# Regrouping loads, transposes and norms at five places of a fused two-layer kernel

## Chip, cores and metric
The kernel runs on one NeuronCore of one Trainium2 chip. The metric is the device time of one execution in microseconds. TensorE is PE in the profile, VectorE is DVE, ScalarE is ACT, GpSimd is POOL and the DMA-issuing SyncE is SP.

## What is computed
Four blocks in a row, each with a residual connection, all in float32, on 2 sequences of 512 tokens of width 256:

```python
x = hidden_states                       # (2, 512, 256)
x = x + delta_rule_attention(layernorm(x))      # 16 heads of 16; q, k, v = silu(conv4(x @ W)); scan over time
x = x + moe0(layernorm(x))              # 8 experts of 176, top 2, plus a shared part of 704
x = x + attention1(layernorm(x))        # 16 query heads, 2 key heads of 128, rotary, tanh soft cap, causal
x = x + moe1(layernorm(x))              # 16 experts of 176, top 6
```

`layernorm` is `(x - mean) / sqrt(var + 1e-5)` over the 256 columns. An expert is `silu(x @ gate) * (x @ up) @ down`.

## The kernel before, in words
All engines run programs written out by hand, with semaphores between them; no planner orders anything, so the order within each engine's function is the order of execution. The 1024 tokens are 8 tiles of 128 rows (`NT`), a half is 4 tiles.

**Start.** `Norm` normalises the tokens. `Norm.dve` does the statistics, the reciprocal and the scaling tile by tile, and each scaled tile counts up `ln_xn`. `Norm.pe_turn` transposes a half on TensorE: for each of the two column blocks (`KD`) four transposes into one bank, all behind one wait for the four tiles. `Norm.act_turn` copies the two banks to `xnT`. Then `attn0.pe` runs the projections (`proj`, L2115): `proj(0)`, `proj(1)`, the second half's `pe_turn`, the betas (L2122), `proj(2)` and on. `Attn0.act` (`pads`) and `Attn0.dve` (`taps`) do the convolution on the projections.

**First mixture.** The shared part and the routed part are separate. The shared part has 17 iterations M (`gate_up` L1281/L1297, `silu` L1552/L1554, `mul` L1674/L1677, `down` L1320). M = 0 to 7 come before the routed blocks, M = `F0B` = 8 to 16 (`F0END` = 17) behind them. Their weights are tiles L of `w_gu` (256 KB) and `w_dn` (128 KB) in a ring of `NW` = 5; SP loads them with `load_gu` (L1063, or two halves at L1061 for the last tile) and `load_dn` (L1070). L = 8 to 11 (`F0B` to `NL0` - 1) are those that M = 8 and later need. The routed part has `NB` = 23 blocks j of 128 token rows. SP reads a row number from `tab` (L1144) and fetches the block's rows from DRAM into `xg`, a ring of three (L1145); block j is fetched once block j - 3 is transposed. TensorE per block: `block_turn` (L953), `block_gate_up` (L967), `block_hidden` (L978), `block_down` (L989); in its loop step j it turns block j + 2, does gate and up of j + 1, hidden of j and down of j - 1. In SP's loop all four weight tiles, nine DMAs, are issued behind block j = 2 and ahead of block 3.

**The norm behind the first mixture.** Norm pieces e = 4 and 5 (`ln_stats`, `ln_std`, `ln_norm`, `ln_turn`, `ln_evac`) are placed among M = 12 to 16. ScalarE's square root (`ln_std`, L490) and its silu use different function tables; `ready` (L1559) runs a one-element activation ahead of time so that the table load comes there.

**Second attention.** 32 heads n (`NH`). TensorE per head: scores (L1461), `turn` of the head before (L1369), `queries` of the next (L1345), `project` of the head before (L1359), probabilities times values (L1502). `owners(J)` reads two offsets for pair J of the second mixture into PE's registers (L778).

**Second mixture.** `NP1` = 32 pairs J of half blocks: `pair_turn` (L728), `pair_hidden` (L756), `pair_gate_up` (L744), `pair_down` (L770) on TensorE, `pair_copy_gu`, `pair_x`, `pair_silu`, `pair_y` on ScalarE. Norm pieces 10 and 11 (for the second half of the tokens) are placed among the pairs; then 25 dense iterations from M = `F1` = 17 follow.

Of the kernel before, what the change touches and what calls it, by code (L numbers as in the profile page):

```python
# [7 lines left out]
P = 128  # L8
# [3 lines left out]
KD = DIM // P  # L12
# [34 lines left out]
ARENA = 39300  # L47
# [21 lines left out]
def build(nc, io):  # L69
    ctx = ExitStack()  # L70
    with ctx:
# [6 lines left out]
        bank = [ctx.enter_context(nc.psum_tensor(f"bank{i}", [P, 512], F32)) for i in range(8)]  # L78
# [20 lines left out]
        arena = sb("arena", [P, ARENA])  # L99
# [7 lines left out]
        s_eps = sem("s_eps")  # L107
# [7 lines left out]
        ln_std, ln_xn, ln_tp, ln_xT = (sem(f"ln_{n}") for n in ("std", "xn", "tp", "xT"))  # L115

        class Norm:
# [29 lines left out]
                    nc.scalar.copy(xnT[:, k, half * HALF:(half + 1) * HALF], bank[q][:]).then_inc(ln_xT, 1)  # L147

            def pe_turn(self, pe, half):
                pe.wait_ge(ln_xn, 4 * (half + 1))  # L150
                for k in range(KD):
                    q = half * KD + k
                    for j in range(4):
                        mm = nc.tensor.transpose(bank[q][:, j * P:(j + 1) * P],
                                                 xn[:, half * 4 + j, k * P:(k + 1) * P], ident[:])
                    mm.then_inc(ln_tp, 1)

        norm = Norm()
        rest = make_rest(nc, io, sem, sb, arena, bank, dict(
            x_sb=x_sb, xn=xn, xnT=xnT, ident=ident, causal_t=causal_t, stats=stats, mv=mv, std=std, rstd=rstd,  # L160
# [26 lines left out]
        @block.gpsimd  # L187
        def _(pool):
            pool.memset(eps_ln[:], EPS).then_inc(s_eps, 1)
            pool.memset(warm[:, 0:2], 0.0).then_inc(s_eps, 1)  # L190
            attn0.pool(pool)
            rest.pool(pool)

# [9 lines left out]

        @block.tensor
        def _(pe):
            pe.wait_ge(s_id.sem, 16)
            norm.pe_turn(pe, 0)
            attn0.pe(pe)
            rest.pe(pe, attn0)
# [8 lines left out]
def make_rest(nc, io, sem, sb, arena, bank, g):  # L218
# [27 lines left out]
    NGRP, NH = BATCH * HKV, BATCH * HQ  # L246
# [229 lines left out]
    class Rest:  # L476
# [632 lines left out]
        def sp(self, sp, attn0):  # L1109
# [31 lines left out]
            for j in range(NB):  # L1141
                if j >= 3:
                    sp.wait_ge(s_bx, j - 2)
                row = sp.value_load(tab[0:1, 0, j:j + 1], min_val=0, max_val=MOE[0][0] * CAP)  # L1144
                sp.dma_start(xg[:, j % 3, :], rows_in[bass.ds(row, P), :]).then_inc(s_cb[j % 3], 16)  # L1145
                if j == 2:
                    for L in range(F0B, F0B + NW - 1):
                        self.load_gu(sp, L)
                        self.load_dn(sp, L)
                if j == 5:  # L1150
                    for L in range(F0B + NW - 1, NL0):
                        self.load_gu(sp, L)
                        self.load_dn(sp, L)
            for n in range(NH):
                if n < NH - 2:
                    sp.wait_ge(s_q, n + 1)
# [215 lines left out]
        def pe(self, pe, attn0):  # L1372
# [66 lines left out]
            for n in range(NH):  # L1439
                grp = n // REP  # L1440
                pe.wait_ge(s_rot, rots(f"q{n}"))
                if n in (4, 5):
                    self.ln_turn(pe, 2 + n)
                if n in K_AT:
                    self.keys(pe, K_AT[n], b_q)
                if n in V_AT:
                    self.values(pe, V_AT[n], b_q)
                if n == 19:
                    self.ln_turn(pe, 9)
                if n == 20:  # L1450
                    self.logits(pe, 2)
                pe.wait_ge(s_qr, rot[f"q{n}"] + 1)
                if n == 0:
                    pe.wait_ge(s_ve, 1)
                for sbank, kts in enumerate([[0], [1, 3], [2]]):
                    if n:
                        pe.wait_ge(s_th, n * 3 - 2 + sbank)
                    for kt in kts:
                        w = SEQ - kt * P
                        o = P_OFF[kt] - 512 * sbank  # L1460
                        mm = nc.tensor.matmul(b_s[sbank][:, o:o + w], kT[:, grp, kt * P:(kt + 1) * P],  # L1461
                                              qr[:, kt * P:SEQ], start=True, stop=True, skip_group_check=True)
                    mm.then_inc(s_sc, 1)
                if n == 18:
                    self.ln_turn(pe, 8)
                if n == 23:
                    self.places1(pe, 0)
                if n:
                    self.turn(pe, n - 1)
                if n in (4, 5):  # L1470
                    pe.wait_ge(ln_xT, 4 + n + 3)
                if n in K_AT:
                    pe.wait_ge(s_rot, rots(f"k{K_AT[n]}"))
                if n in V_AT:
                    pe.wait_ge(s_ve, V_AT[n] + 1)
                if n == 18:
                    pe.wait_ge(ln_xT, 4 + 9)
                if n == 19:
                    pe.wait_ge(ln_xT, 4 + 10)
                if n == 20:  # L1480
                    pe.wait_ge(s_sub, 3)
                if n == 23:
                    pe.wait_ge(s_pl, RD1[0])
                if n < NH - 1:
                    self.queries(pe, n + 1)
                else:
                    self.pair_turn(pe, 0)
                if n == NH - 2:
                    offs = [owners(J) for J in range(3)]
                if n:  # L1490
                    self.project(pe, n - 1)
                else:
                    self.values(pe, 1, b_y[1])
                if n == NH - 1:
                    self.pair_turn(pe, 1)
                pe.wait_ge(s_p, n * 2 + 2)
                for pair in range(2):
                    for t in range(2):
                        qb = pair * 2 + t
                        for kt in range(qb + 1):  # L1500
                            o = P_OFF[kt] + (qb - kt) * P
                            mm = nc.tensor.matmul(b_o[pair][:, t * (DH + 1):(t + 1) * (DH + 1)],  # L1502
                                                  pr[:, o:o + P], v[:, grp, kt, :],
                                                  start=(kt == 0), stop=(kt == qb))
                    mm.then_inc(s_pv, 1)
# [59 lines left out]
        def act(self, act, attn0):  # L1565
# [29 lines left out]
            for M in range(F0B + 1, F0END):  # L1595
                self.silu(act, M)
                if M == F0END - 4:
                    self.ready(ACT.Sqrt)
                    self.ln_std(act, 4)
                if M == F0END - 3:  # L1600
                    self.ready(ACT.Sqrt)
                    self.ln_std(act, 5)
                if M == F0END - 2:
                    self.ln_evac(act, 4)
            self.ln_evac(act, 5)
            self.ready(ACT.Tanh)
            self.v_evac(act, 0, b_s[0])
# [31 lines left out]
            for J in range(NP1):  # L1639
# [4 lines left out]
                    self.pair_silu(act, J + 1)  # L1644
                if J:
                    self.pair_y(act, J - 1)
                if J == 5:
                    self.ln_std(act, 10)
                if J == 6:
                    self.ln_std(act, 11)  # L1650
                if J == 9:
                    self.ln_evac(act, 10)
# [53 lines left out]
        def dve(self, dve, attn0):  # L1706
# [38 lines left out]
            for M in range(F0B, F0END):  # L1745
# [8 lines left out]
                if M == F0END - 3:  # L1754
                    self.add_rows(dve, 1)
                    self.ln_stats(dve, 5)
                if M == F0END - 2:
                    self.ln_norm(dve, 5)
            dve.wait_ge(s_cs, 48)
            dve.wait_ge(s_k, 1)  # L1760
# [1230 lines left out]
```

## Time and profile before

| | |
|---|---|
| median of 3 runs | 836.53 us (835.92 to 839.29) |
| the profiled execution | 836.49 us |
| its span, first to last instruction | 834.7 us |
| mean granted TensorE clock | 0.991 |
| PE busy | 787.2 us (94%) |
| DVE busy | 482.1 us (58%) |
| ACT busy | 360.4 us (43%) |
| POOL busy | 218.4 us (26%) |

The span is the time inside the core; the rest of the execution's time, 1.8 us, lies around it. Busy time of PE counts matmul records; one float32 matmul is two records here, a transpose is one. "Idle before <- X" in a row is idle time of that engine just ahead of the instruction and what ended it.

### The profile page before, as it was taken

What the parts mean: (1) busy time and instruction counts of PE and PEld (TensorE: products, weight loads), DVE (VectorE), ACT (ScalarE), POOL (GpSimd) and SP (SyncE); (2) the same over time, 40 slices, a digit from 0 to 9 for tenths busy, and PEclk for the clock granted to TensorE, in tenths of its full rate; (3) what the DMA queues carried; (4) which work ended last, traced back from release to release, by engine and by line L of the source; (5) the groups of instructions that cost most, each with busy time, mean ns of one, the idle gap of its engine ahead of it and who ended that gap; (6) DMA issues with size and microseconds to landing.
All of it is one profiled execution on the core that took longest, in us unless ns stands there. A gap on an engine that the chain in (4) does not pass through costs nothing.

```text
span 834.7 us, 14393 instructions
## 1 busy us (share of the span) xinstructions
PE 787.2 (94%) x4825; PEld 545.6 (65%) x4825; DVE 482.1 (58%) x1167; ACT 360.4 (43%) x755; POOL 218.4 (26%) x318
## 2 busy tenths in 40 slices
PE   5988799879989998899999999999999999999998
PEld 3576566665657776577777777777764545455557
DVE  5999866766622225865564575967645463324443
ACT  3988777646213324343323343232347666211111
POOL 3644654111610015111211211217712333200000
PEclk9998999999999999999999999999999999999999
DMA  4001790083343312034443232223333433284431
GB/s 145 2 1 29 220 309 1 3 209 101 102 139 103 106 60 82 13 103 135 122 131 93 69 102 69 61 54 99 119 71 114 141 96 110 88 278 126 127 126 50
DMA packets 95807, 85.72 MB, mean 103 GB/s; under 512 B 34792, under 2 KB 84456, under 8 KB 95736
## 3 DMA queue, kind: packets, MB, share of 16 engines
q1 hardware_dynamic: 88200, 70.05, 28.9%
q0 software_dynamic: 4224, 11.74, 4.0%
q10 hardware_dynamic: 3312, 3.02, 1.1%
q8 instruction: 41, 0.67, 0.3%
q14 instruction: 30, 0.25, 0.1%
HBM read 57.02 MB, written 26.71 MB: 100 GB/s over the span
## 4 chain that ended last, share of the span: by engine, by line
PE 79%; DVE 10%; ACT 6%; issue 3%; DMA 1%; SPq 1%; POOL 0%; ACTq 0%; DVEq 0%; POOLq 0%
PE bank L1502 9%; PE bank L1461 8%; PE bank L1320 7%; PE bank L1359 7%; PE bank L1345 6%; PE bank L1281 6%; PE bank L1297 6%; PE bank L744 4%; PE bank L770 3%; PE bank L967 3%; PE bank L2330 3%; PE bank L989 2%; ACT arena L2387 2%; PE bank L2287 2%; PE bank L2314 2%
## 5 line engine op out<-in xcount | busy, mean ns | idle before, releaser
L1619 ACT ACTIVATE arena<-bank 128x512 f32<-128x512 f32 (+1 forms) x96 | 46.8, 525 | 142.7 <-PE bank L1461 142.7
L1243 POOL TENSOR_TENSOR arena<-arena,causal_t 128x256 f32<-128x256 f32 x64 | 45.3, 729 | 208.5 <-ACT arena L1624 207.5
L1502 PEld LDWEIGHTS bank<-arena 128*128 128x128 f32 x640 | 76.2, 191 | 3.9 <-POOL arena L1243 2.3
L1502 PE MATMUL bank<-arena 128*128 128x129 f32 x640 | 77.0, 275 | 1.5 <-POOL arena L1243 1.5
L1461 PE MATMUL bank<-arena 128*128 128x512 f32 (+3 forms) x256 | 74.5, 434 | 1.4 <-DVE arena L1697 1.4
L1554 ACT ACTIVATE arena<-bank 128x512 f32<-128x512 f32 (+1 forms) x39 | 20.2, 520 | 120.7 <-PE bank L1281 111.9
L1320 PE MATMUL bank<-arena 128*128 128x256 f32 (+1 forms) x272 | 66.2, 382 | 3.5 <-DVE arena L1677 3.4
L1281 PE MATMUL bank<-xnT,arena 128*128 128x512 f32 (+1 forms) x168 | 65.9, 514 | 0.0
L1320 PEld LDWEIGHTS bank<-arena 128*128 128x128 f32 (+1 forms) x272 | 50.9, 190 | 21.8 <-issue 10.8
L1359 PEld LDWEIGHTS bank<-arena 128*128 128x128 f32 x256 | 48.3, 190 | 21.6 <-issue 13.6
L1359 PE MATMUL bank<-arena 128*128 128x256 f32 x256 | 60.8, 380 | 1.4 <-issue 0.9
L1345 PE MATMUL bank<-arena 128*128 128x512 f32 x128 | 60.5, 595 | 1.2 <-DVE arena L1695 0.8
L1297 PE MATMUL bank<-xnT,arena 128*128 128x512 f32 (+1 forms) x156 | 61.5, 516 | 0.0
L1461 PEld LDWEIGHTS bank<-arena 128*128 128x128 f32 x256 | 41.3, 191 | 27.0 <-issue 18.5
L1679 DVE TENSOR_TENSOR arena<-arena,bank 128x512 f32<-128x512 f32 (+1 forms) x25 | 15.6, 623 | 68.0 <-PE bank L1297 68.0
L851 POOL DMA_INDIRECT ret<-arena,ridx x32 | 30.7, 960 | 77.0 <-ACT arena L818 60.3
L1693 DVE TENSOR_TENSOR arena<-bank,arena 64x512 f32<-64x512 f32 x36 | 25.0, 693 | 36.7 <-PE bank L1345 26.2
L1297 PEld LDWEIGHTS bank<-xnT,arena 128*128 128x128 f32 x156 | 29.6, 190 | 25.3 <-issue 23.8
L744 PE MATMUL bank<-arena 128*64 (+1 forms) x256 | 44.9, 472 | 0.0
L1704 DVE COPY arena<-bank 128x256 f32<-128x256 f32 x64 | 24.1, 418 | 34.5 <-PE bank L1369 30.8
L2330 PE MATMUL bank<-w,arena 128*128 128x128 f32 x248 | 35.5, 286 | 7.2 <-DVE w L2863 3.3
L1281 PEld LDWEIGHTS bank<-xnT,arena 128*128 128x128 f32 x168 | 31.2, 190 | 16.5 <-issue 14.0
(297 smaller groups left out, 1489.6 us busy)
## 6 DMA issues: line engine op xcount, KB each, us to landing
arena<-in_w_gu SPq DMA_DIRECT2D x44, 256.0 KB, 3.3
rows_in<-place SPq DMA_DIRECT2D x5, 1664.0 KB, 14.6
arena<-in_w_dn SPq DMA_DIRECT2D x34, 128.0 KB, 3.5
rows<-arena SPq DMA_DIRECT2D x8, 544.0 KB, 4.4
arena<-in_w_dn SPq DMA_DIRECT2D x24, 176.0 KB
arena<-in_wq SPq DMA_DIRECT2D x32, 128.0 KB
arena<-in_wo SPq DMA_DIRECT2D x32, 128.0 KB
arena<-rows SPq DMA_DIRECT2D x32, 128.0 KB, 2.0
```

Of the source, the lines that this page charges most:

```text
L744: mm = nc.tensor.matmul(p_gu[J % 2][u * HR:(u + 1) * HR, 0:2 * FE].rearrange("p (y n) -> p y n", y=2), pxT[:, J % 2, k, u * HR:(u + 1) * H ...
L851: nc.gpsimd.indirect_dma_start(ret[h], bass.IndirectOffsetOnAxis(ap=ridx[:, h, j:j + 1], axis=0), py[J % NY], None).then_inc(s_ret, 16)
L1243: nc.gpsimd.tensor_tensor(blocks, blocks, causal_t[:].unsqueeze(1).to_broadcast([P, 2, P]), ALU.mult).then_inc(s_p, 1)
L1281: mm = nc.tensor.matmul(ring(M)[0][:, 0:n], (w_gu, w_gu1)[s][:, slot_of(M), k * P:(k + 1) * P], xnT[:, k, cols], start=(k == 0), stop=(k = ...
L1297: mm = nc.tensor.matmul(ring(M)[1][:, 0:n], (w_gu, w_gu1)[s][:, slot_of(M), (KD + k) * P:(KD + k + 1) * P], xnT[:, k, cols], start=(k == 0 ...
L1320: mm = nc.tensor.matmul(Y[s][half][l // 2][:, (l % 2) * DIM:(l % 2 + 1) * DIM], (hh, hh1)[s][rows, M % 3, j * P:(j + 1) * P], (w_dn, w_dn1 ...
L1345: mm = nc.tensor.matmul(b_q[:], wq[:, n % 2, k, :], xnT2[:, k, b * SEQ:(b + 1) * SEQ], start=(k == 0), stop=(k == KD - 1))
L1359: mm = nc.tensor.matmul(b_y[t // 2][:, (t % 2) * DIM:(t % 2 + 1) * DIM], oT[:, t * P:(t + 1) * P], wo[:, n % 2, :], start=first and t % 2 ...
L1461: mm = nc.tensor.matmul(b_s[sbank][:, o:o + w], kT[:, grp, kt * P:(kt + 1) * P], qr[:, kt * P:SEQ], start=True, stop=True, skip_group_chec ...
L1502: mm = nc.tensor.matmul(b_o[pair][:, t * (DH + 1):(t + 1) * (DH + 1)], pr[:, o:o + P], v[:, grp, kt, :], start=(kt == 0), stop=(kt == qb))
L1619: nc.scalar.activation(th[:, sbank * 512:sbank * 512 + w], b_s[sbank][:, 0:w], ACT.Tanh, scale=SCALE / SOFTCAP).then_inc(s_th, 1)
L2330: mm = nc.tensor.matmul(sacc[h][:, j * P:(j + 1) * P], kq[:, u, hq * P:(hq + 1) * P], ub[s][:, hq, :], start=False, stop=True, skip_group_ ...
```

## The change
It has five parts. (1) At the start GpSimd also zeroes 384 columns of the arena (`still`), and TensorE runs nine 128x256 matmuls on them into bank 7, which nobody reads, ahead of everything else. (2) `Norm.pe_turn` waits for each tile singly and transposes both its column blocks, in place of waiting for four. (3) SP issues the four weight tiles for M = 8 and later one behind each of the blocks j = 6, 7, 8 and 9, in place of all behind block 2. (4) On TensorE the offsets of the pairs 0, 1 and 2 are read in heads 28, 29 and 30, one pair each, in place of all in head 30. (5) The square roots are moved: that of piece 5 from M = 14 to behind M = 16's silu, and `ln_norm(5)` to behind mul(16); those of pieces 10 and 11 both stand in J = 6, in place of J = 5 and 6.

```diff
             def pe_turn(self, pe, half):
-                pe.wait_ge(ln_xn, 4 * (half + 1))
-                for k in range(KD):
-                    q = half * KD + k
-                    for j in range(4):
-                        mm = nc.tensor.transpose(bank[q][:, j * P:(j + 1) * P],
+                for j in range(4):
+                    pe.wait_ge(ln_xn, 4 * half + j + 1)
+                    for k in range(KD):
+                        mm = nc.tensor.transpose(bank[half * KD + k][:, j * P:(j + 1) * P],
                                                  xn[:, half * 4 + j, k * P:(k + 1) * P], ident[:])
-                    mm.then_inc(ln_tp, 1)
-
+                        if j == 3:
+                            mm.then_inc(ln_tp, 1)
+
+        still = arena[:, ARENA - 3 * P:]
...
             pool.memset(warm[:, 0:2], 0.0).then_inc(s_eps, 1)
+            pool.memset(still, 0.0).then_inc(s_eps, 1)
...
         def _(pe):
+            pe.wait_ge(s_eps, 3)
+            for _ in range(9):
+                nc.tensor.matmul(bank[7][:, 0:256], still[:, 0:P], still[:, P:3 * P], start=True, stop=True)
             pe.wait_ge(s_id.sem, 16)
...
                 sp.dma_start(xg[:, j % 3, :], rows_in[bass.ds(row, P), :]).then_inc(s_cb[j % 3], 16)
-                if j == 2:
-                    for L in range(F0B, F0B + NW - 1):
-                        self.load_gu(sp, L)
-                        self.load_dn(sp, L)
-                if j == 5:
-                    for L in range(F0B + NW - 1, NL0):
-                        self.load_gu(sp, L)
-                        self.load_dn(sp, L)
+                if F0B <= F0B + j - 6 < NL0:
+                    self.load_gu(sp, F0B + j - 6)
+                    self.load_dn(sp, F0B + j - 6)
...
-                if n == NH - 2:
-                    offs = [owners(J) for J in range(3)]
+                if n == NH - 4:
+                    offs = []
+                if n >= NH - 4 and len(offs) < 3:
+                    offs.append(owners(len(offs)))
...
                 if M == F0END - 4:
                     self.ready(ACT.Sqrt)
                     self.ln_std(act, 4)
-                if M == F0END - 3:
+                if M == F0END - 2:
+                    self.ln_evac(act, 4)
+                if M == F0END - 1:
                     self.ready(ACT.Sqrt)
                     self.ln_std(act, 5)
-                if M == F0END - 2:
-                    self.ln_evac(act, 4)
             self.ln_evac(act, 5)
...
-                if J == 5:
+                if J == 6:
                     self.ln_std(act, 10)
-                if J == 6:
                     self.ln_std(act, 11)
...
                     self.ln_stats(dve, 5)
-                if M == F0END - 2:
+                if M == F0END - 1:
                     self.ln_norm(dve, 5)
```

## Rows read from the trace of the kernel before

**Rows 1.** The page's chain of work that ended last, by engine.
```profile
PE 79%; DVE 10%; ACT 6%; issue 3%; DMA 1%; SPq 1%; POOL 0%; ACTq 0%; DVEq 0%; POOLq 0%
```
**Rows 2.** Timeline, TensorE alone, 7 to 26 us: start, us.
```profile
7.83 1.94 PE L154 MATMUL bank<-ident,xn 128*128 128x128 f32 x8 [7.83 <-DVE xn L135]
10.44 5.56 PE L2115 MATMUL bank<-xnT,w 128*128 128x512 f32 x8 [0.68 <-ACT xnT L147]
15.84 1.04 PE L154 MATMUL bank<-ident,xn 128*128 128x128 f32 x8
...
18.42 7.97 PE L2115 MATMUL bank<-xnT,w 128*128 128x512 f32 x18
```
**Rows 3.** Timeline, all engines, 0 to 22 us.
```profile
0.81 0.32 POOL L2576 MEMSET place<- 128x256 f32 x1
...
3.09 0.43 SPq L177 DMA_DIRECT2D w<-in_w  x1
...
6.30 1.38 DVE L135 TENSOR_SCALAR xn<-x_sb,mv,rstd 128x256 f32<-128x256 f32 x4
...
8.95 0.58 ACT L147 COPY xnT<-bank 128x512 f32<-128x512 f32 x1 [2.90 <-PE bank L154]
```
**Rows 4.** DMA issues, 0 to 30 us: KB, median us to landing.
```profile
w<-in_w SPq DMA_DIRECT2D x1, 512.0 KB, 6.3
```
**Rows 5.** Timeline, all engines, 226 to 262 us.
```profile
241.61 1.23 SPq L1061 DMA_DIRECT2D arena<-in_w_gu  x2
...
242.82 0.38 PE L978 MATMUL bank<-ident,arena 128*88 128x128 f32 x2
...
244.24 17.75 SPq L1145 DMA_DIRECT2D arena<-rows_in  x9
...
246.42 0.69 PE L953 MATMUL bank<-ident,arena 128*128 128x128 f32 x2 [3.21 <-DMA arena<-rows_in]
...
250.57 0.38 PE L953 MATMUL bank<-ident,arena 128*128 128x128 f32 x2
...
253.06 0.38 PE L953 MATMUL bank<-ident,arena 128*128 128x128 f32 x2
```
**Rows 6.** Two stretches: busy time by engine, granted clock, DMA share, GB/s.
```profile
246.00:248.00 2.00, 1.58 (x4) 1.15 (x5) 0.00 (x0) 0.37 (x1) 0.00 (x0) 0.58 0.39 116
249.00:250.00 1.00, 1.00 (x5) 0.71 (x4) 0.17 (x1) 0.32 (x1) 0.00 (x0) 0.63 0.25 85
```
**Rows 7.** Timeline, all engines, 300 to 350 us.
```profile
323.97 0.29 ACT L490 ACTIVATE std<-mv,eps_ln 128x2 f32<-128x2 f32 x1 [3.03 <-DVE mv L485]
...
324.28 1.28 ACT L1554 ACT_TABLE_LOAD   x1
...
325.99 0.42 DVE L1677 TENSOR_TENSOR arena<-arena,bank 128x256 f32<-128x256 f32 x1 [2.06 <-ACT arena L1554]
...
326.52 0.73 DVE L500 TENSOR_SCALAR xn<-x_sb,mv,rstd 128x256 f32<-128x256 f32 x2
...
327.44 0.60 PE L510 MATMUL bank<-ident,xn 128*128 128x128 f32 x4
...
329.02 1.99 PE L1328 MATMUL bank<-arena 128*128 128x512 f32 x4
```
**Rows 8.** The chain of work, 560 to 640 us: start, us, what.
```profile
605.80 0.88 issue
...
633.23 1.33 PE bank L744 x8
...
636.02 1.33 PE bank L744 x8
```
**Rows 9.** Line 778, 596 to 626 us: ns min/median/max, first and last start.
```profile
L778 PEldq TENSOR_LOAD <-tab x11: 302/307/522, 602.2 to 625.6; - x11
```
**Rows 10.** The chain of work, 632 to 660 us: start, us, what.
```profile
641.20 1.28 ACT L812
...
646.39 1.33 PE bank L744 x8
```

## Prediction
> **What bounds the kernel now.** I read the page's chain first, then the chain in order of time, then the timeline wherever the chain leaves TensorE. The chain lies on TensorE for 79% of the span, on DVE for 10% and on ACT for 6% [rows 1], so an edit pays only where TensorE waits, or works at its low clock, on that chain. Each of the five edits touches such a place. At the start TensorE first works at 7.83 and its first eight projection records take 5.56 us, where eighteen later ones of the same shape take 7.97 [rows 2], 0.44 each. In the routed blocks TensorE idles 3.21 us until the rows of block 3 land [rows 5]. Behind the first mixture it waits for a silu that ScalarE could only do after a table load [rows 7]. In head 30 there are 0.88 us in which nothing but TensorE's own sequencer is busy [rows 8]. Among pairs 5 to 8, gate and up of a pair come later than their steady beat [rows 8, 10].
>
> **Weights behind blocks 6 to 9: 4.9 us.** SP is still issuing the last weight tile at 241.61 and gets to block 3's rows at 244.24; they land at about 246.4 (3.21 us of TensorE's idle time ends there, and 0.69 us of transposes start at 246.42) [rows 5]. TensorE had block 0's hidden transposes done by 242.82 + 0.38 = 243.20 [rows 5] and would have turned block 3 next. SP's nine weight issues are what made the read late: without them it goes out some 5 us earlier, since block 0 was turned before 239. So the turn of block 3 moves from 246.42 to 243.20, 3.2 us. The idle time also cost the clock: the granted clock averages 0.58 in 246 to 248 and 0.63 in 249 to 250 [rows 6], the low level of 1.2 GHz for most of it, right behind 3.21 us without work. From the turn of block 4 to that of block 5 it is 253.06 - 250.57 = 2.49 us [rows 5], the steady beat, and the same from 3 to 4 was 250.57 - 246.42 = 4.15. That is 1.66 us more, so in all 3.22 + 1.66 = 4.9 us. I take 4.9; nearly all of it should come, as no other engine is behind at that point.
>
> What the loads cost in their new place: per block SP then has one row read and two weight issues. From 241.61 two issues take 1.23 us, the worst case; even with 1.2 us more for the other tile and under 1 us for the row read this is about 3.2 us for one block and some 2 us for the other three, against a beat of 2.49. A row read is allowed three blocks ahead, 7.5 us, and needs about 2.1 us to land, so up to 4 us of lateness is covered. M = 8 needs the first of these weights some 45 us later. If that cover were gone, each late block would cost what block 3 costs now.
>
> **The norm behind the mixture: 1.5 us.** Now: statistics ready, std(5) at 323.97, silu's table reloaded 324.28 to 325.56, silu(15), mul(15) at 325.99, norm(5) at 326.52, turn(5) at 327.44, and the keys at 329.02 [rows 7]. After the change silu(15) and silu(16) come before the square root, while DVE is still in add_rows and statistics; the sqrt table load of 1.28 us follows silu(16) at about 322.8 and is over by 324.1, hidden behind the same DVE work, which ends just before 323.97. Then mul(15) and mul(16), 0.42 each [rows 7], run 323.95 to 324.8 while std(5) is done beside them; reciprocal and norm start at 325.0, turn(5) 0.9 later at 325.9 instead of 327.44. The 1.58 us from turn(5) to the keys stay. Gain 1.5 us. The tanh table, which silu's covers now, must be loaded again: 1.28 us on ScalarE while TensorE does keys and values for 3 us, nothing. Bounds: 0 if add_rows comes later still, 1.54 + 1.0 if the wait ahead of it shrinks as well.
>
> **Offsets: 1.0 us.** Six register loads stand in a row ahead of `project`; the first is at 602.2 [rows 9], TensorE's queued matmuls last until 605.80, and 0.88 us are left bare [rows 8]. So six take 4.5 us or about 0.75 each. Two at a time take 1.5 us and there are 3.6 us of queued work to hide them. In head 28 they may wait a little for the table that DVE writes at the end of head 27; by the same offsets that leaves some 0.3 us. Gain 0.9 to 1.1, minus 0 to 0.4 in head 28. I take 1.0.
>
> The Trainium skill ("TensorE: Matmul & The Clock Gate", the table at its head) gives TensorE a queue of 64 instructions against 8 on the other engines. By it the sequencer could run up to 64 instructions ahead; here it was 3.6 us ahead, which is what lets two loads hide.
>
> **Square roots of pieces 10 and 11: 1.7 us.** The steady beat of a pair is 636.02 - 633.23 = 2.79 [rows 8]. The fourth gate-up after 636.02 starts at 646.39 or later [rows 10]; three beats would give 644.4, so the two interruptions cost 2.0 us by then and about 0.3 more behind. Each is two table loads of 1.28 and a square root, 2.85 us on ScalarE; the first eats ScalarE's slack and the second, one pair later, falls in full: silu's reload is at 641.20 for the first [rows 10]. Together the two roots cost one 3.15 us interruption in place of 2.85 twice, and I leave 0.6 us of it on the path: gain 1.7, between 1.3 and 2.3.
>
> The Trainium skill ("ScalarE: Activation LUTs", on ACT_TABLE_LOAD) counts for every switch of set 1.28 us of load and another 1.38 us of drain. Here the silu that reloads its table ends its load at 325.56 and DVE's product of that silu starts at 325.99 [rows 7], so the drain is not to be seen. By the page two switches saved would free 5.3 us of ScalarE instead of 2.6, still no more than the 2.3 us that are lost.
>
> **The start: 2.4 us.** A zeroing of 256 columns takes 0.32 us on POOL [rows 3], so 384 take some 0.45 and TensorE can start at 1.3. Nine matmuls are 18 records of 256 columns; a 512-column record takes 0.44 at the full clock [rows 2], so these take 0.22, 0.43 at the low one: 7.7 us in all if the clock stays low, to 9.0. The profile's clock column has no entry for this stretch, so the durations must say it: eight projection records from 10.44 to 15.84 [rows 2] fit 3.85 us at 0.88 and the rest at 0.44, a rise to 2.4 GHz at about 14.3, 3.9 us after the projections began and 6.5 after the first transposes at 7.83. With 3.3 us (246.42 to where [rows 6] put the second rise) as the short end, the clock rises between 4.6 and 7.8 and the zeros end halfway between that and 9.0: 6.8 to 8.4, middle 7.6. The eight transposes take 1.04 us at the full clock against 1.94 [rows 2], the last tile being there at 6.30 + 1.38 [rows 3]: done at 8.0 to 9.4. Two copies of 0.58 [rows 3] now follow each other: projections from 9.4 to 10.7. The weights land at 3.09 + 6.3 = 9.4 [rows 3, 4], no later. Against 10.44 this is little or nothing, but the eight records then take 3.5 in place of 5.4: the second half's transposes move from 15.84 to 12.9 to 14.2. Gain 1.7 to 2.9; I take 2.4. It lasts, as from there TensorE, ScalarE and DVE hand over to each other without a fixed time; POOL's zeroing and the loads end well ahead. Worst: the clock doesn't rise before the transposes, which then end at 9.0 + 1.94 = 10.9, projections at 12.1 and 5.4 us long: 1.7 us lost.
>
> The Trainium skill (same TensorE page, "PE-mode transpose") says that transposes don't count as busy for the clock gate as matmuls do. The first rise agrees: it came 6.5 us after the transposes began but 3.9 after the projections did. It speaks against this edit, because transposes and copies, some 2.3 us, now stand between the zeros and the projections.
>
> **Sum.** 4.9 + 1.5 + 1.0 + 1.7 + 2.4 = 11.5 us. The profiled execution took 836.49 (span 834.7 and 1.8 around it), the median of the runs is 836.53: 836.5 - 11.5 = 825.0. Nothing I found refills a gap: all later work is released by TensorE's own progress.
>
> **Rivals.**
> (a) The start gives nothing or costs: the clock is not up, or falls again during transposes and copies. Then the projections keep their 5.4 us from 9.9 (gain 0.4), or start at 12.1 (loss 1.7): 827 to 829. For it: no record of zeros exists in this trace, and the low clock behind 3.21 us of idle time [rows 5, 6]. Against: here the gap is shorter. Chance 0.17.
> (b) The reordered square roots give back what they take (the norm waits for two products, or the pairs slip once in full): 1.5 + 1.7 lost, 828. For it: ScalarE has little slack per pair. Chance 0.15.
> (c) Slower than before: weights and row reads share one queue. Data of up to 384 KB now lie ahead of each of the rows of blocks 7 to 10; if every such read were as late as block 3's is now, that is 4 x 4.9 = 19.6 us lost against 11.5 gained: 844.6. It decides from about 3 us a block. Against: block 3's rows, behind nine such DMAs, landed 2.1 us after their issue [rows 5]. Chance 0.02. The Trainium skill ("DMA: Bandwidth & Descriptors", HWDGE ordering) has each DMA engine take descriptors in ring order, which is this rival's mechanism; the row just named does not bear it out.
> (d) Part (3) does what it says but the sum of the rest is under 2 us, through several small waits that the trace does not show: 830 to 832.5. Chance 0.06.
> The forecast, all five within their bounds: 0.60, 822.5 to 826.5 as its own range.
>
> **From these the numbers.** Range 821.5 to 830.0: the low end adds the upper bounds of the start, the norm and the pairs (0.5 + 1.0 + 0.6) and 1.3 for a low-clock stretch elsewhere that need not recur; the high end covers (a) and (b). About 0.5% (4.2 us) is what this measurement can tell. Faster by more than that: all but (c) and some of (d), 0.94; within it 0.04; slower 0.02.
>
> **What would show it.** TensorE's first record at 1.3 us, 18 of them, the last half at 0.22; projections from about 10 at 0.44 each; no idle of TensorE before block 3's turn and a beat of 2.49 from block 2 on, with no low clock there; keys about 1.5 us sooner after the last silu; no bare stretch ahead of `project` in head 30; one table-load pair in place of two around J = 6. The prediction is wrong if the block stage keeps a wait for row reads at blocks 7 to 10, or if the projections still run at 0.88.

## The result and the profile after

| | before | after |
|---|---|---|
| median | 836.22 us (4 runs, 834.40 to 839.29) | 824.97 us (4 runs, 823.24 to 826.65) |
| the profiled execution | 836.49 us | 823.24 us |
| its span | 834.7 us | 821.4 us |

The ratio of after to before is 0.9867, 95% interval [0.9846, 0.9888]: faster, by 1.3%. The medians differ by 11.25 us, the two profiled executions by 13.25 us, as after's is the fastest of its four. The forecast of 825.0 us was right for the whole. Two of its terms (the norm and the start) came out otherwise, and there are three effects that it did not have: a table load that fell away, a loss in head 26, and a wait that comes and goes.

The page of the changed kernel gives the chain by engine, to be held against [rows 1]:

```profile
PE 74%; DVE 9%; issue 6%; ACT 5%; POOL 4%; DMA 2%; SPq 0%; ACTq 0%; DVEq 0%; POOLq 0%
```

PE's share fell from 79% to 74% although TensorE's busy time is 788.0 us against 787.2, and "issue" doubled. I could not put that down to one place, and did not read the change from this row. I read it by laying the two traces beside each other: the start of each TensorE record in before less that of the same record in after. That difference, called the shift, changes for good at seven places only:

| place | before less after, us | step |
|---|---|---|
| up to the first routed block's turn | 0 to 2.76 | +2.8 |
| routed blocks | to 7.76 | +5.0 |
| M = 12 to 16 and the norm | to 10.32 | +2.6 |
| head 0 | to 11.60 | +1.3 |
| heads 26 and 27 | to 10.66 | -0.9 |
| head 30 | to 11.78 | +1.1 |
| pairs 5 to 8 | to 13.25 | +1.5 |

**Start.** TensorE alone, 0 to 20 us, answering [rows 2], and the zeroing on POOL, answering [rows 3]:

```profile
1.29 5.56 PE L210 MATMUL bank<-arena 128*128 128x256 f32 x18 [1.29 <-POOL arena L192]
6.99 1.32 PE L153 MATMUL bank<-ident,xn 128*128 128x128 f32 x8
9.37 3.70 PE L2116 MATMUL bank<-xnT,w 128*128 128x512 f32 x8 [1.05 <-ACT xnT L147]
12.91 1.04 PE L153 MATMUL bank<-ident,xn 128*128 128x128 f32 x8
```
```profile
0.81 0.42 POOL L192 MEMSET arena<- 128x384 f32 x1
```

Eighteen zero records take 5.56 us, less than 18 x 0.43: the granted clock rose to 2.4 GHz at 4.2, during them. The transposes are released singly, the projections start 1.07 us sooner, and eight of their records take 3.70 us instead of 5.56. The second half's transposes start 2.93 us sooner (12.91 against 15.84), above the 2.4 that I took and at the upper bound of 2.9.

**Routed blocks.** Timeline of after, 234 to 262 us, answering [rows 5]; then a window of it, answering [rows 6]:

```profile
240.10 0.38 PE L983 MATMUL bank<-ident,arena 128*88 128x128 f32 x2
240.32 0.38 PE L958 MATMUL bank<-ident,arena 128*128 128x128 f32 x2
...
241.82 0.43 SPq L1068 DMA_DIRECT2D arena<-in_w_gu  x1
...
242.30 0.43 SPq L1075 DMA_DIRECT2D arena<-in_w_dn  x1
242.81 0.38 PE L958 MATMUL bank<-ident,arena 128*128 128x128 f32 x2
...
243.92 0.35 SPq L1150 DMA_DIRECT2D arena<-rows_in  x1
...
245.30 0.38 PE L958 MATMUL bank<-ident,arena 128*128 128x128 f32 x2
...
247.79 0.38 PE L958 MATMUL bank<-ident,arena 128*128 128x128 f32 x2
```
```profile
245.00:248.00 3.00, 3.00 (x17) 2.26 (x16) 1.10 (x4) 0.97 (x4) 0.00 (x0) 1.00 0.60 152
```

Block 3's turn at 240.32 directly follows the hidden transposes; the turns of blocks 4, 5 and 6 follow 2.49 us apart while SP issues weights between row reads; the granted clock stays at 1.00 (2.4 GHz).

**Norm.** Timeline of after, 300 to 325 us, answering [rows 7]:

```profile
314.20 0.38 ACT L1554 ACTIVATE arena<-bank 64x256 f32<-64x256 f32 x1 [0.28 <-PE bank L1281]
...
314.59 1.28 ACT L1561 ACT_TABLE_LOAD   x1
314.70 0.25 DVE L490 BATCH_NORM_AGGREGATE mv<-stats 128x2 f32<-128x6 f32 x2
...
316.00 0.28 ACT L495 ACTIVATE std<-mv,eps_ln 128x2 f32<-128x2 f32 x1
316.31 0.17 DVE L500 RECIPROCAL rstd<-std 128x2 f32<-128x2 f32 x1 [0.60 <-ACT std L495]
...
317.37 0.66 PE L515 MATMUL bank<-ident,xn 128*128 128x128 f32 x4 [0.62 <-DVE xn L505]
...
318.67 1.28 ACT L1561 ACT_TABLE_LOAD   x1
319.02 1.98 PE L1328 MATMUL bank<-arena 128*128 128x512 f32 x4
```

The statistics are ready at 314.95, both products of DVE at 315.70, and the square root only at 316.00, because its table load began at 314.59 and not earlier. The load that I had called hidden is what DVE waits for (0.60 us of idle time).

Whether it is hidden depends on when the statistics are ready, and that varies between executions. Earlier in this stage DVE's first add of the shared part waits, by the profile mostly for the end of a `down`: 1.64 us in before, 0.45 in after. In three other executions with the new order (`changed_again`, `loads_all_at_6`, `offsets_back`, all below) it waits 1.54 to 1.63 us; there the load is over in time and DVE is idle 0.03 us instead of 0.60. From the last statistics instruction to the keys it is 5.24 us in before, 4.22 in after and 3.57 in those three.

**Offsets and square roots of the pairs.** Line 783's register loads on TensorE's queue, answering [rows 9]; then after's chain in head 30, where [rows 8] had the bare issue, and at the place of [rows 10]:

```profile
L783 PEldq TENSOR_LOAD <-tab x6: 306/311/477, 576.4 to 592.2; - x6
```
```profile
593.42 1.72 PE bank L1345 x4
595.14 1.73 PE bank L1359 x8
...
627.01 1.33 PE bank L749 x8
...
631.15 0.28 ACT std L495
...
633.14 1.33 PE bank L749 x8
```

The loads now lie between 576.4 and 592.2, and the 0.88 us of bare issue ahead of `project` are gone: L1359 follows L1345 directly. Among the pairs both roots stand behind one another and one interruption is left: 627.01 to 633.14 is two beats of 2.79 and 0.55 more, where before lost 2.0.

### The profile page after: what moved, and what is told of

The parts are those of the page before. It is cut to its first block, busy times and chain, and to the rows that moved or that the text cites. A ratio compares the mean times of both kernels' runs of the same rounds, so it can differ in the third digit from the quotient of the medians.

```text
span 821.4 us, 14427 instructions
## 1 busy us (share of the span) xinstructions
PE 788.0 (96%) x4843; PEld 548.4 (67%) x4843; DVE 481.8 (59%) x1167; ACT 356.7 (43%) x752; POOL 218.2 (27%) x319
## 4 chain that ended last, share of the span: by engine, by line
PE 74%; DVE 9%; issue 6%; ACT 5%; POOL 4%; DMA 2%; SPq 0%; ACTq 0%; DVEq 0%; POOLq 0%
PE bank L1504 8%; PE bank L1461 7%; PE bank L1359 6%; PE bank L1345 6%; PE bank L1281 6%; PE bank L1297 5%; PE bank L1320 5%; PE bank L749 5%; PE bank L972 3%; PE bank L775 3%; PE bank L2331 3%; PE bank L994 2%; ACT arena L2388 2%; PE bank L2288 2%; PE bank L2315 2%
## 5 line engine op out<-in xcount | busy, mean ns | idle before, releaser
L1359 PEld LDWEIGHTS bank<-arena 128*128 128x128 f32 x256 | 48.5, 190 | 20.2 <-issue 12.4
L1345 PE MATMUL bank<-arena 128*128 128x512 f32 x128 | 60.5, 596 | 0.9 <-DVE arena L1696 0.5
L1359 PE MATMUL bank<-arena 128*128 128x256 f32 x256 | 60.7, 380 | 0.5 <-DVE arena L1705 0.5
```

The source lines that it names most:

```text
L1345: mm = nc.tensor.matmul(b_q[:], wq[:, n % 2, k, :], xnT2[:, k, b * SEQ:(b + 1) * SEQ], start=(k == 0), stop=(k == KD - 1))
L1359: mm = nc.tensor.matmul(b_y[t // 2][:, (t % 2) * DIM:(t % 2 + 1) * DIM], oT[:, t * P:(t + 1) * P], wo[:, n % 2, :], start=first and t % 2 ...
```

## The experiments

Each kernel was timed beside the kernel before on the same chip. The chips differ (before's median is 835.17 to 837.41 us on them), so a ratio, which is to the kernel before, says more than a median. "Shift" is again the difference in start of the same TensorE record, here against after's trace.

### One part undone at a time

**The weights back behind block 2** (`loads_back`):

```diff
-                if F0B <= F0B + j - 6 < NL0:
-                    self.load_gu(sp, F0B + j - 6)
-                    self.load_dn(sp, F0B + j - 6)
+                if j == 2:
+                    for L in range(F0B, NL0):
+                        self.load_gu(sp, L)
+                        self.load_dn(sp, L)
```

> The changed kernel with its four weight tiles again issued all behind block 2; all else as changed. My theory (the row read of block 3 stood behind nine weight issues): 4.9 us slower than the changed kernel, 830 us, with TensorE idle some 3.2 us ahead of block 3's turn, matmuls at half speed for 3.4 us behind it, and the steady beat of 2.49 us from block 4 on. Rival (the read was late because rows were not yet written, and the weights' place matters only through bandwidth): under 1.5 us slower.

Measured: 829.31 us (8 runs), ratio 0.9923 [0.9898, 0.9947]. The wait and the low clock are back, in its timeline (234 to 262) and its window:

```profile
240.37 0.38 PE L983 MATMUL bank<-ident,arena 128*88 128x128 f32 x2
241.57 20.50 SPq L1150 DMA_DIRECT2D arena<-rows_in  x10
243.91 0.44 PE L958 MATMUL bank<-ident,arena 128*128 128x128 f32 x2 [3.16 <-DMA arena<-rows_in]
```
```profile
245.00:248.00 3.00, 3.00 (x9) 1.95 (x8) 0.67 (x2) 0.32 (x1) 0.00 (x0) 0.50 0.27 80
```

The shift grows by 5.1 us here (0.27 to 5.35), 3.3 of idle time and 1.8 of 1.2 GHz. Part (3) is worth what was worked out. It is the only part whose ratio, when undone, has its whole interval above that of the changed kernel.

**All four tiles behind block 6** (`loads_all_at_6`, the same lines with `j == 6`):

> The changed kernel with its nine weight DMAs all behind block 6 in place of two behind each of blocks 6 to 9. My prediction says up to 4 us of lateness of a row read are covered by the ring of three. The nine issues take about 4.7 us of SP and the row read has waited for its block's turn before, so block 7's rows come some 1 us late at most: 0 to 1 us slower than the changed kernel. Rival (c), data ahead in the shared queue decide: over 3 us slower, with low clock behind the idle time.

Measured: 825.55 us (5 runs), ratio 0.9853 [0.9829, 0.9878]. Its timeline (234 to 262) shows one wait of 1.30 us:

```profile
254.62 6.92 SPq L1150 DMA_DIRECT2D arena<-rows_in  x5
...
257.51 0.44 PE L958 MATMUL bank<-ident,arena 128*128 128x128 f32 x2 [1.30 <-DMA arena<-rows_in]
```

So moving the burst to where rows are already three blocks ahead removes most of the 4.9 us, and spreading it removes the remaining 1.45 in the trace, somewhat more than the 0 to 1 us expected. The median does not resolve that 1.45.

**The norm back** (`norm_back`): `ready(ACT.Sqrt)` and `ln_std(5)` again at M = 14, ahead of silu(15), and `ln_norm(5)` behind mul(15).

> The changed kernel with the square root of piece 5, its ready() and norm(5) in their old places. By my prediction's step 1.5 us slower than the changed kernel. The changed kernel's trace says more: the keys came about 2.1 us sooner and head 0 lost a 1.28 us table load for the exponential, so 2.3 to 3.4 us slower, about 828, with a table load at the first exponential again. Rival (add_shared started 1.1 us sooner in the changed kernel's profiled execution by chance): then 1.0 of the 2.1 does not come back and it is 2.3.

Measured: 826.62 us (6 runs), ratio 0.9884 [0.9858, 0.9911]. The interval overlaps the changed kernel's. In the trace the shift grows by 1.0 in the norm (from piece 4's transposes to the keys it is 7.33 us, in after 6.32) and by another 1.27 in head 0, 2.3 in all, which is what the rival of the expectation asked for. The first is what the regrouping gives in an execution with the short wait of DVE (0.47 us here); the second has another cause, next below.

**The square roots of 10 and 11 back** (`roots_back`): `ln_std(10)` again in J = 5.

> The changed kernel with the square roots of pieces 10 and 11 again in J = 5 and J = 6. My theory: 1.55 to 1.7 us slower than the changed kernel, about 826.6, and the two interruptions cost TensorE 2.3 us in all. Rival (the slack of ScalarE's queue takes both in): no slower.

Measured: 825.43 us (5 runs), ratio 0.9873 [0.9844, 0.9901]. The shift grows by 1.5 us among the pairs (0.70 to 2.17), against 1.55 to 1.7 expected. The median hardly moved; that it is worth 1.5 us rests on the trace alone.

**The offsets back** (`offsets_back`): all six loads again in head 30.

> The changed kernel with all six register loads again in head 30. My theory: 0.9 to 1.1 us slower than the changed kernel, and the chain again shows about 0.9 us of issue ahead of the projection in head 30. Rival (some later wait gives it back): no slower, with TensorE waiting elsewhere ahead of the first pair.

Measured: 824.84 us (5 runs), ratio 0.9853 [0.9829, 0.9877], no slower than the changed kernel. In its chain the bare issue is back in head 30 and costs 1.0 us (the shift goes from 5.47 to 6.46), as worked out:

```profile
600.61 0.75 issue
```

But this execution lacks the 0.9 us that after loses in head 26 (6.41 to 5.47), so the two cancel. The one is not the price of the other; what happens in head 26 comes further below.

### The 1.3 us in head 0

In before ScalarE loads a table in head 0, in after it does not. The kernel before with one word changed (`before_exp_set`) asks for the exponential's table behind the last silu, in place of tanh's:

```diff
-            self.ready(ACT.Tanh)
+            self.ready(ACT.Exp)
```

> The kernel before with one word changed: the one-element activation behind the norm of the first mixture is an exponential in place of a tanh. Theory for the part of the gain that I had not foreseen: silu's table also serves tanh but not exp, so the kernel before reloads in head 0 in the open; the set that is loaded for exp serves tanh as well. Then this kernel is 1.2 us faster than before, with a table load near 328 and none near 341. Rival: tanh needs its own set and the load only moves to the first tanh, no faster.

Measured: 836.14 us (12 runs) against 837.41, ratio 0.9983 [0.9965, 1.0002]. The medians differ by what was expected, but the interval reaches 1, so the traces have to show it. ScalarE's timeline, of before and then of this kernel:

```profile
324.28 1.28 ACT L1554 ACT_TABLE_LOAD   x1
...
328.56 0.21 ACT L1559 ACTIVATE warm<-warm 128x1 f32<-128x1 f32 x1
...
341.64 1.28 ACT L1624 ACT_TABLE_LOAD   x1
342.93 1.27 ACT L1624 ACTIVATE arena<-arena 128x1280 f32<-128x1280 f32 x1
```
```profile
329.48 1.28 ACT L1559 ACT_TABLE_LOAD   x1
330.77 0.20 ACT L1559 ACTIVATE warm<-warm 128x1 f32<-128x1 f32 x1
...
342.48 1.27 ACT L1624 ACTIVATE arena<-arena 128x1280 f32<-128x1280 f32 x1
```

In before, tanh at 328.56 needs no load: silu's table serves it. The exponential at 342.93 then needs one, on the path. With one word changed the load comes at 329.48, hidden, and this kernel's lag behind before, 0.8 us until then, turns into a lead of 0.4: 1.25 us in head 0. In after the square root stands last, so tanh must be loaded anew at 318.67, and what is loaded serves the exponential too. The Trainium skill ("ScalarE: Activation LUTs", "Table sets: the hidden batching unit") lists tanh in two sets, that of exp and another; the traces agree, and the saving is 1.25 us.

**The square root ahead of silu(16)** (`root_before_silu16`) takes after, asks for the exponential's table, and tries for the 0.60 us left in the norm:

```diff
                 if M == F0END - 2:
+                    self.ready(ACT.Sqrt)
                     self.ln_evac(act, 4)
-                if M == F0END - 1:
-                    self.ready(ACT.Sqrt)
                     self.ln_std(act, 5)
             self.ln_evac(act, 5)
-            self.ready(ACT.Tanh)
+            self.ready(ACT.Exp)
```

and `ln_norm(5)` behind mul(15).

> The changed kernel with the square root of piece 5 between silu(15) and silu(16), norm(5) ahead of mul(16) again, and an exponential in place of the tanh as the one-element activation behind it, so that the reload of silu's table costs nothing later. If TensorE's wait ahead of piece 5's transposes is for the table load that follows silu(16): keys 0.7 us sooner than in the changed kernel, and no table load in head 0; about 824.5. If silu(16)'s reload then ends the chain: no gain or up to 1 us of loss.

Measured: 823.74 us (6 runs, 822.60 to 825.82), ratio 0.9836 [0.9803, 0.9869]; the changed kernel run beside it (`changed_third`) has 0.9868 [0.9833, 0.9904]. Its timeline, 300 to 330 us:

```profile
312.82 1.28 ACT L1561 ACT_TABLE_LOAD   x1
...
315.36 0.30 ACT L495 ACTIVATE std<-mv,eps_ln 128x2 f32<-128x2 f32 x1 [0.57 <-DVE mv L490]
315.67 1.28 ACT L1554 ACT_TABLE_LOAD   x1
...
316.97 0.60 PE L515 MATMUL bank<-ident,xn 128*128 128x128 f32 x4
317.85 1.13 PE L1320 MATMUL bank<-arena 64*128 64x256 f32 x4 [0.28 <-DVE arena L1674]
318.90 1.98 PE L1328 MATMUL bank<-arena 128*128 128x512 f32 x4
```

The square root's load is hidden now, but silu(16) needs its own again at 315.67, and TensorE waits for that product instead. The keys start 0.12 us before after's, in a stage whose first transposes came 0.38 later, so 0.5 in the stage; the spans are 821.5 and 821.4. It has the lowest median of all kernels here, but no place in its trace explains more than 0.5 us and the intervals overlap: not shown to be faster than the changed kernel.

### What the start is worth

**Without the zeros** (`no_zeros`; the nine matmuls and the zeroing are left out, tiles are still turned singly):

```diff
-        still = arena[:, ARENA - 3 * P:]
...
-            pool.memset(still, 0.0).then_inc(s_eps, 1)
...
-            pe.wait_ge(s_eps, 3)
-            for _ in range(9):
-                nc.tensor.matmul(bank[7][:, 0:256], still[:, 0:P], still[:, P:3 * P], start=True, stop=True)
```

> The changed kernel without the nine zero products and without the zeroing of their 384 columns; tiles still turned singly. My theory (the gain at the start is the clock): 2.4 to 3.0 us slower than the changed kernel, 827.5 to 828, the first eight projection records again at 0.86 to 0.88 us each until about 14.2 us. Rival (turning tiles singly is what gained): no more than 0.5 us slower, because the transposes then start at about 6.9 us.

Measured: 825.02 us (5 runs), ratio 0.9865 [0.9837, 0.9894], the same as with them. TensorE alone, 0 to 20 us:

```profile
6.71 1.94 PE L153 MATMUL bank<-ident,xn 128*128 128x128 f32 x8 [6.71 <-DVE xn L135]
9.61 5.96 PE L2111 MATMUL bank<-xnT,w 128*128 128x512 f32 x8 [0.95 <-ACT xnT L147]
15.41 1.04 PE L153 MATMUL bank<-ident,xn 128*128 128x128 f32 x8
```

The local effect is as worked out: the projections take 5.96 us instead of 3.70, and the second half's transposes come 2.5 us later. My theory, that this lasts to the end, then asked for a median about 2.4 us higher, and it was not. The rival was that something later takes it back, differently in each execution. The changed kernel again (`changed_again`, `changed_third`), this one again (`no_zeros_again`), and one with neither zeros nor single turns (`no_zeros_grouped`: `Norm.pe_turn` as before as well) were run for it.

> The changed kernel itself, as the base for the others of this call: 824.5 to 825.5 us. If the time at which the clock rises at the start is not fixed, its profile shows another time for it than 4.2 us, between 4 and 7.8, and the start gains between 1.7 and 3.0 us accordingly.

> The changed kernel, as the base of this call: 824 to 826 us. By theory B its executions spread over some 5 us, and each one whose mean granted clock is lower is longer.

> The changed kernel without the nine zero products, a second time, now beside the changed kernel on one chip. The traces say that the zeros save 2 us up to the second half's transposes; the medians of the first call say nothing is saved. Theory A (the gain stays): 1.5 to 2.5 us slower than the changed kernel in the same call. Theory B (the zeros only move the instants at which the clock can change, and further low stretches in the first attention, seen near 99, 106 and 183 us in two of the profiles with zeros and in none without, take it back in some executions): medians within 1 us, the lowest time of the changed kernel lower by 1 to 2 us, and its highest higher.

> The changed kernel without the zero products and with the four tiles of a half again behind one wait, that is with the start of the kernel before. My theory, from the traces: the first projection at 10.44 us in place of 9.60, so turning tiles singly is worth 0.8 us by itself, and the clock rises near 14.2 us as without zeros: 0.5 to 0.9 us slower than without zeros alone. Rival (the projections wait for their weights anyway): no difference.

| kernel | zeros | median, us (runs) | ratio |
|---|---|---|---|
| after | yes | 824.97 (4) | 0.9867 [0.9846, 0.9888] |
| `changed_again` | yes | 825.44 (6) | 0.9868 [0.9840, 0.9895] |
| `changed_third` | yes | 826.42 (6) | 0.9868 [0.9833, 0.9904] |
| `no_zeros` | no | 825.02 (5) | 0.9865 [0.9837, 0.9894] |
| `no_zeros_again` | no | 825.58 (6) | 0.9864 [0.9827, 0.9901] |
| `no_zeros_grouped` | no | 825.23 (6) | 0.9863 [0.9829, 0.9897] |

Six ratios within 0.0005; all executions together have a median of 826.1 with the zeros (16) and of 825.4 without (17). By `no_zeros_grouped` the whole start, zeros and single turns, gives nothing that the medians can tell. The first projection starts at 10.62 there against 9.97 in `no_zeros_again`, but the turn of block 0 comes at 238.36 against 238.68, so the 0.5 to 0.9 us that I expected of the single turns was not seen either; the rival, no difference, is what was measured.

The single executions differ in spread: with the zeros they run from 823.24 to 829.60, nearly evenly; without them 14 of 17 lie between 824.44 and 825.73, and the other three at 827.77, 827.92 and 830.29. That is weaker than it seems. In the last set of runs the rival's forecast of a lower lowest and a higher highest time with the zeros failed (824.37 to 829.09, without them 824.46 to 830.29), a lower mean clock did not always go with a longer time (826.26 us at 0.989, 826.59 at 0.992), and the kernel before, which has no zeros, ran from 836.10 to 842.24 on one chip. A clearer difference is seen at a fixed record, the turn of routed block 0, up to which all these kernels differ in the start alone. It starts, in the nine profiled executions with zeros, at 235.33, 235.60, 235.72, 236.01, 236.83, 237.18, 238.37, 240.96 and 241.11; in the five without, those of before included, at 238.07, 238.09, 238.36, 238.68 and 238.84. So the zeros save 3 us at best and 1.5 at the median (236.83 against 238.36), and cost 2.7 at worst. Windows show where the time goes, 88 to 97 for after and for `changed_third`, and 98 to 111 for `offsets_back`, where after has a granted clock of 1.00 throughout, in this order (us, busy time of PE, PEld, DVE, ACT and POOL with counts, granted clock, DMA share, GB/s):

```profile
88.00:97.00 9.00, 5.42 (x68) 2.67 (x68) 8.24 (x23) 7.56 (x20) 7.96 (x16) 1.00 0.84 271
```
```profile
88.00:97.00 9.00, 6.98 (x52) 3.75 (x56) 8.08 (x22) 7.25 (x17) 4.93 (x10) 0.62 0.59 178
```
```profile
98.00:104.00 6.00, 5.07 (x56) 3.38 (x56) 3.06 (x12) 3.54 (x11) 6.00 (x14) 0.72 1.08 378
104.00:111.00 7.00, 5.14 (x49) 3.43 (x46) 4.05 (x9) 2.28 (x10) 1.83 (x5) 0.76 1.06 363
```

Between the projections and the first mixture TensorE is busy only part of the time, and there the granted clock falls to 1.2 GHz for some us. Where it falls differs from one execution to the next. In after it falls at 48.5, at 72.4 and nowhere else before the end; in `changed_third` also from 89.4 to 96.2, where its lag behind after grows from 2.1 to 3.1 us; in `offsets_back` and `loads_all_at_6` at 99 and 106, where some 4.3 us go; in `changed_again` at 183, where 1.4 us go. The five executions without zeros have low stretches between 48 and 55 (one of them not even that) and from 76 to 83, and no other before the routed blocks. With the zeros the first rise comes at 4.2 to 7.5 us, in all nine ahead of the first transpose; without them at 14.2 to 15.0. That the different rise is what moves the later falls is inferred; the falls themselves are in the traces.

## Why the prediction came out right, point by point

- **Weights, 4.9 us:** right. Measured 5.0 between the traces and 5.1 in the experiment that undoes it, with the two parts (idle time, low clock) as worked out. The cover of three blocks held for tiles issued one at a time; for all four in one piece (`loads_all_at_6`) it did not quite, and that cost 1.45 us. Rival (c) did not occur.
- **Norm, 1.5 us:** the order was right, a size was not. Measured 1.0 (5.24 to 4.22 us from the statistics to the keys). The step that failed in after is "the sqrt table load of 1.28 us follows silu(16) ... hidden behind the same DVE work": silu(16) came only 0.75 us before the statistics, so the load ended 0.92 us after them. The forecast had taken before's long wait of DVE (1.64 us) for fixed. In the three executions of the new order that have that wait, the load is hidden as forecast and the stretch is 1.67 us shorter.
- **"The tanh table ... must be loaded again: ... nothing":** wrong in the good direction. The load that comes anew at 318.67 replaces one at 341.64 on the path, 1.25 us. The row of that second load is in before's timeline; I had priced the table added, and had not asked which one became unnecessary.
- **Offsets, 1.0 us:** right in the trace (1.1, and 1.0 undone). The 0 to 0.4 us that I allowed for head 28 did not occur.
- **Square roots of the pairs, 1.7 us:** measured 1.5 between the traces and 1.5 undone. The 2.0 us lost and the 0.6 left (0.55 measured) were right; the "about 0.3 more behind" was not there. The gate-up at 646.39, three beats and 2.0 us behind 636.02, is the third behind it and not the fourth. The drain behind a table load, which I had doubted, is not seen in after either: a load at 309.71 ends at 310.99 and its silu starts at 311.00.
- **Start, 2.4 us:** the mechanism was right (2.9 at the second half's transposes, 2.8 at block 0), and the step that failed is "It lasts". By the six medians the start gives nothing that can be measured, about what rival (a) gives, but by another cause: the clock was up in time. Over the profiled executions 1.5 us are left at block 0 at the median, as the clock falls elsewhere, and head 26 takes 0.9 of these. The rule that transposes don't count as busy for the clock gate ("TensorE: Matmul & The Clock Gate", "PE-mode transpose", in the Trainium skill) was set against this edit; here the clock stayed up through transposes and copies (the eight projection records behind them take 3.70 us in after), so it did not decide.
- **The sum.** In after's execution 2.8 + 5.0 + 1.0 + 1.3 - 0.9 + 1.1 + 1.5 = 11.8 of the 13.25 us. Of the other 1.45 about 1.2 is DVE's wait of 1.64 us in before against 0.45 in after: from before to after this stretch up to the keys gives 2.25 us, from `norm_back`, which has the old order and the short wait, only 1.0. The changed kernel shows both waits, 1.54 in `changed_again` and 0.39 in `changed_third`, so the change is not its cause. 0.3, ahead of the queries of head 0, stays unassigned. That the forecast met the median to 0.1 us is thus partly luck: the table (+1.25) makes up for the norm (-0.5) and part of the start, and the interval of the ratio is 1.8 us wide on either side. Rival (d), which did not come, was stated as 830 to 832.5; its own terms give 829.6 to 831.6.

**Head 26.** POOL there waits for a scatter to land before the next one, and the mask behind it comes late. Its timeline in after and in `offsets_back`:

```profile
563.76 1.12 POOL L846 DMA_INDIRECT rows<-arena,sidx  x1 [1.56 <-DMA rows<-arena,sidx]
```
```profile
568.78 1.01 POOL L846 DMA_INDIRECT rows<-arena,sidx  x1 [0.16 <-issue]
```

The wait of 1.4 to 2.1 us is in all eight executions that have both the zeros and the early offsets, and in none of the six that lack one of them. What lengthens it is a fetch of instructions. The page gives these a DMA queue of their own:

```profile
q8 instruction: 41, 0.67, 0.3%
```

These are 41 transfers of 16 KB. After's trace has 10,687 records of TensorE and its sequencer, some 260 for each transfer, and no other engine has nearly as many, so I take them for TensorE's. The trace also keeps queue, start and end of every transfer (no row above shows them). Counted from the start of the last scatter ahead of the wait, the eight executions have a fetch that starts at 1.72 to 2.08 us and lasts 0.93 to 1.67, and the scatter's last write ends at 3.01 to 4.15. In after the fetch runs from 561.49 to 562.42 and the write ends at 562.43. In the other six the last write ends at 2.05 to 2.10.

The offsets have no part in this: the fetch starts at 2.08 in after and at 2.10 in `offsets_back`, each time at TensorE's record 7,606, and in `offsets_back` the last write is just through. The zeros do have one. All nine executions with them have the fetch at 1.7 to 2.1, and in the five without them the nearest one comes at 3.8 to 7.4. The zeros put 36 records ahead of TensorE's program (10,687 against 10,651); that this is what moves the fetch is inferred. The loss in head 26 is 0.9 us between after and each kernel without zeros (2.72 to 1.77 in `no_zeros`).

## What to carry to other kernels

When DMA issues of one queue sit ahead of a read that is due, move them to where the reads run furthest ahead, and spread them: here that was 5 of some 12 us, and the largest term and the clearest in the medians. When moving an activation, write down the table before and after it and see which later load appears or disappears, not only the one that is moved. A gain of 2 to 3 us from an earlier clock rise should be counted at a later fixed record over several executions, since falls of the clock further on may move as well. Instructions added at one place can also move an instruction fetch onto a transfer that something waits for, far behind them.

## What was not expected of the hardware

- Which table serves tanh depends on what was loaded before: none needed behind silu (328.56 in before), and a 1.28 us load behind a square root (318.67 in after) that the exponential then shares.
- The same kernel shows the low granted clock at different places in different executions (89.4 to 96.2 in one, 183.2 to 186.6 in another, neither in a third), and the turn of block 0 is spread over 5.8 us in nine executions with zero products at the start, over 0.8 in five without.
- One semaphore wait behind a `down` took 0.2 to 0.5 us in nine executions and 1.5 to 1.6 us in five, both of them in the same code. Its cause is open.
- A 16 KB fetch of instructions held back the last write of a scatter that was in flight by 0.9 to 2.0 us (3.01 to 4.15 us after its start against 2.05 to 2.10).
